# Two LSTM layers on one core: own activations for the gates g and i, biases of g and i copied in by ScalarE

## The reference

```python
def step(carry, xp_t):
    prev_h, prev_c = carry
    h_bar = xp_t + prev_h @ Wh                 # xp = x @ Wx + b
    i = jax.nn.sigmoid(h_bar[:, 0:Hdim])
    f = jax.nn.sigmoid(h_bar[:, Hdim:2 * Hdim])
    o = jax.nn.sigmoid(h_bar[:, 2 * Hdim:3 * Hdim])
    g = jnp.tanh(h_bar[:, 3 * Hdim:4 * Hdim])
    next_c = f * prev_c + i * g
    next_h = o * jnp.tanh(next_c)
    return ((next_h, next_c), next_h)
...
x = x + attention(lstm1(x, cond))     # theta, phi, g projections; (theta phi^T / sqrt(128)) g
x = x + ffn(lstm2(x, cond))           # relu(h W1 + b1) W2 + b2
```

## Time and profile before

| | us |
|---|---|
| runs, median of 3 | 435.31 |
| runs, lowest and highest | 435.30, 435.46 |
| profiled execution, first to last instruction (span) | 431.1 |
| TensorE matmul busy in it | 413.9 (96%) |
| VectorE busy | 282.0 (65%) |
| ScalarE busy | 192.1 (45%) |
| TensorE weight loads busy | 301.4 (70%) |

### The profile page before, as it was taken

The page is one execution under the profiler, slowest core; times in us unless marked ns, Lnnn a source line. Parts: engine busy times, 40 slices in busy tenths (PEclk is TensorE's granted clock), DMA queues, the critical chain, the costliest instruction groups (busy, mean ns, idle before and its releaser), DMA issues.

```text
span 431.1 us, 14329 instructions
## 1 busy us (share of the span) xinstructions
PE 413.9 (96%) x5020; PEld 301.4 (70%) x5020; DVE 282.0 (65%) x1702; ACT 192.1 (45%) x1132; POOL 7.8 (2%) x20
## 2 busy tenths in 40 slices
PE   8999999999999999999999999999999999999996
PEld 5767666666766666666689777777777777777775
DVE  6766666666666666666668766666667666666664
ACT  3565444445444444544445433343443434343342
POOL 7000000000000000000000000000000000000000
PEclk9999999999999999999999999999999999999999
DMA  5011011111001111000000100000000000000000
GB/s 180 10 20 20 13 10 18 18 18 18 13 5 18 18 18 18 16 2 14 14 14 2 27 21 6 12 18 20 18 18 0 18 18 18 18 17 1 18 18 12
DMA packets 11694, 8.19 MB, mean 19 GB/s; under 512 B 1097, under 2 KB 11129, under 8 KB 11674
## 3 DMA queue, kind: packets, MB, share of 16 engines
q1 hardware_dynamic: 10874, 6.17, 7.2%
q0 software_dynamic: 512, 1.22, 0.9%
q10 hardware_dynamic: 288, 0.52, 0.4%
HBM read 2.87 MB, written 1.05 MB: 9 GB/s over the span
## 4 chain that ended last, share of the span: by engine, by line
PE 83%; ACT 7%; DVE 5%; issue 3%; DMA 1%; SPq 0%; DVEq 0%
PE fbank L420 19%; PE bankV L400 14%; PE gibank L414 9%; PE bankU L389 6%; PE bankV L414 5%; PE gibank L377 4%; PE bankY L619 4%; PE bankU L612 3%; DVE cell L990 3%; PE bankV L484 3%; ACT scan L802 3%; PE bankY L479 2%; ACT fgate L795 2%; PE gibank L383 2%; PE bankU L512 2%
## 5 line engine op out<-in xcount | busy, mean ns | idle before, releaser
L420 PEld LDWEIGHTS fbank<-ring,whf 128*128 128x128 f32 x508 | 76.6, 188 | 91.7 <-DVE ring L998 88.1
L795 ACT ACTIVATE fgate<-fbank 128x16 f32<-128x16 f32 x254 | 46.5, 183 | 153.5 <-PE fbank L420 153.2
L420 PE MATMUL fbank<-ring,whf 128*128 128x16 f32 x508 | 98.2, 269 | 6.1 <-DVE ring L998 0.7
L987 DVE TENSOR_TENSOR scan<-fgate,cell 128x16 f32<-128x16 f32 x254 | 45.1, 178 | 77.5 <-ACT fgate L795 75.4
L400 PE MATMUL bankV<-warm_x,zeros 128*128 128x512 bf16 x294 | 93.0, 379 | 0.0
L990 DVE TENSOR_TENSOR_SCAN cell<-scan 128x48 f32<-128x48 f32 x256 | 68.2, 267 | 12.0 <-ACT scan L802 1.1
L809 ACT ACTIVATE cell<-cell 128x16 f32<-128x16 f32 x256 | 43.0, 168 | 67.9 <-DVE cell L990 67.8
L998 DVE TENSOR_TENSOR ring<-cell,ogate_h 128x16 f32<-128x16 f32 x256 | 44.7, 174 | 41.8 <-ACT cell L809 41.6
L414 PEld LDWEIGHTS gibank<-h_hi,wh_parts 128*128 128x128 f16 x1016 | 65.4, 117 | 0.0
L414 PE MATMUL gibank<-h_hi,wh_parts 128*128 128x16 f16 x1016 | 62.1, 169 | 0.0
L414 PE MATMUL gibank<-h_lo,wh_parts 128*128 128x16 f16 x1016 | 62.0, 169 | 0.0
(11 more groups left out here) (182 smaller groups left out, 505.6 us busy)
## 6 DMA issues: line engine op xcount, KB each, us to landing
rows_t<-rows SPq DMA_DIRECT2D x16, 128.0 KB
x_rows<-in_x_dram SPq DMA_DIRECT2D x17, 64.0 KB
out_dram<-y_sb SPq DMA_DIRECT2D x16, 64.0 KB
xres<-x2T SPq DMA_DIRECT2D x15, 64.0 KB, 1.9
xin<-x2T SPq DMA_DIRECT2D x14, 64.0 KB, 1.9
w<-in_L_ffn_W_dram POOLq DMA_DIRECT2D x2, 256.0 KB, 4.1
wh<-in_L_cond_Wh_dram ACTq DMA_DIRECT2D x1, 256.0 KB, 2.7
wx<-in_L_cond_Wx_dram ACTq DMA_DIRECT2D x1, 256.0 KB, 3.6
```

The source lines that it names most:

```text
L420: nc.tensor.matmul(step_out(p, t, GF), whf[layer][:], ring[:, (s - 1) % STEPS, :], start=False, stop=True, skip_group_check=True).then_inc ...
L795: nc.scalar.activation(fgate[:], fbank[p][:, NB * t:NB * t + NB], ACT.Sigmoid, scale=1.0 / Z_UNIT).then_inc(f_done[layer], 1)
L987: nc.vector.tensor_tensor(out=fc_slots, in0=fgate[:], in1=c_psum, op=ALU.mult).then_inc(scan_inputs[layer], 1)
```

## The change

The gates g and i get banks of their own (`gbank`, `ibank`), each with both halves in it. ScalarE does a tanh for g and a sigmoid for i, with a semaphore from TensorE for each (`g_ready`, `i_ready`), and the tanh of c has no scale. The scan runs over two elements for each sequence: slots hold 0 and g to multiply by, i and f*c to add, so that state = 0 * state + i, then state = g * i + f c. Nothing is doubled in the set-up any more.

Since both halves of g and i are in one bank, their biases come as those of o did: TensorE spreads them once for each layer into 128 columns, ScalarE keeps them (`seeds`) and copies three of them in for the other half at t = 0 (`seed`). TensorE waits for the last of the three (`seeded`) at t = 1, now behind the f matmul and ahead of the passes of g. The projections of g and i wait for `o_done` as that of o does; in layer 1 that of o moves from t = 3 to t = 4, where a filler goes. `WARM2` has 9 fillers for each chunk in place of 14.

```diff
-    WARM2 = [0, 2, 1, 2, 2, 2, 2, 3]
+    WARM2 = [0, 2, 1, 1, 2, 2, 1, 1]
+    SEEDED = [GG, GI, GO]
@@ tiles
-        gibank = [ps("gibank0"), ps("gibank1")]
-        cell = ps("cell")
+        gbank, ibank, cell = ps("gbank"), ps("ibank"), ps("cell")
-        c_scan, tanhc = cell[:, 0:3 * NB], cell[:, 3 * NB:4 * NB]
-        scan_mul, scan_add = scan[:, 0:3 * NB], scan[:, 3 * NB + 1:6 * NB + 1]
-        gi_slots = scan[:, 2:6 * NB + 2].rearrange("p (g b k) -> p g b k", g=2, k=3)[:, :, :, 0]
+        c_scan, tanhc = cell[:, 0:2 * NB], cell[:, 2 * NB:3 * NB]
+        scan_mul, scan_add = scan[:, 0:2 * NB], scan[:, 2 * NB:4 * NB]
+        g_slots = scan_mul.rearrange("p (b k) -> p b k", k=2)[:, :, 1]
+        i_slots = scan_add.rearrange("p (b k) -> p b k", k=2)[:, :, 0]
+        fc_slots = scan_add.rearrange("p (b k) -> p b k", k=2)[:, :, 1]
+        def shared_cols(p, g):
+            if g == GO:
+                return bankV[:, (2 + p) * P:(3 + p) * P]
+            return (gbank if g == GG else ibank)[:, p * P:(p + 1) * P]
@@ TensorE, step
+                if after_seeds is not None:
+                    pe.wait_ge(seeded, after_seeds)
                 pe.wait_ge(hi_ready[layer], count)
-                passes(h_hi, [GG, GI])
+                passes(h_hi, GG, (0, 1))
+                passes(h_hi, GI, (0,))
                 pe.wait_ge(lo_ready[layer], count)
-                passes(h_lo, [GG, GI]).then_inc(gi_ready[layer], 1)
+                passes(h_lo, GG, (0, 1)).then_inc(g_ready[layer], 1)
+                passes(h_hi, GI, (1,))
+                passes(h_lo, GI, (0, 1)).then_inc(i_ready[layer], 1)
-                if seeded is not None:
-                    pe.wait_ge(o_seeded, seeded)
@@ TensorE, layer 1 beside the steps
-                if t in (0, 1):
-                    for g in (GATES[0:1], GATES[1:3])[t]:
-                        bias_gate(int(last), 1 - p, g)
+                if t == 0:
+                    bias_gate(int(last), 1 - p, GF)
                 if s == 1 and first:
                     pe.wait_ge(o_done[0], 2)
-                    bias_gate(0, 1, GO).then_inc(o_bias_ready, 1)
+                    for g in SEEDED:
+                        bias_gate(0, 1, g).then_inc(bias_spread, 1)
+                if t in (3, 4):
+                    for g in (SEEDED[0:2], SEEDED[2:3])[t - 3]:
+                        pe.wait_ge(seeded, i * 2 + (p + 1))
+                        pe.wait_ge(o_done[0], i * STEPS + (s + 1))
...
-                elif t not in (0, 3) and not (first and s == 1):
+                elif t not in (0, 3, 4) and not (first and s == 1):
                     add_zeros(1 + (t == 1), 0, i * STEPS + (s + 1))
@@ TensorE, layer 1, step 7 of the first turn
-                    nc.tensor.matmul(bankU[:, 0:P], bias[1][:, gate_cols(GO)], ones[:], start=True, stop=True
-                                     ).then_inc(o_bias_ready, 1)
+                    for k, g in enumerate(SEEDED):
+                        nc.tensor.matmul(bankU[:, k * P:(k + 1) * P], bias[1][:, gate_cols(g)], ones[:],
+                                         start=True, stop=True).then_inc(bias_spread, 1)
@@ TensorE, loop of layer 2
-                    if t in (2, 3, 6):
-                        g = {2: GF, 3: GG, 6: GI}[t]
-                        bias_gate(1, 1 - p, g)
-                        project_gate(1, 1 - p, g, xin[:, 1 - p, :])
-                    if t == 7:
-                        pe.wait_ge(o_seeded, c + (NCH + 1))
+                    if t == 2:
+                        bias_gate(1, 1 - p, GF)
+                        project_gate(1, 1 - p, GF, xin[:, 1 - p, :])
+                    if t in (3, 6, 7):
+                        pe.wait_ge(seeded, c + (NCH + 1))
                         pe.wait_ge(o_done[1], i * STEPS + (s + 1))
-                        project_gate(1, 1 - p, GO, xin[:, 1 - p, :]).then_inc(x2_projected, 1)
+                        last = project_gate(1, 1 - p, {3: GG, 6: GI, 7: GO}[t], xin[:, 1 - p, :])
+                        if t == 7:
+                            last.then_inc(x2_projected, 1)
@@ ScalarE
-                act.wait_ge(gi_ready[layer], n1)
-                nc.scalar.activation(gi_slots,
-                                     gibank[p][:, 2 * NB * t:2 * NB * (t + 1)].rearrange("p (g b) -> p g b", g=2),
-                                     ACT.Tanh, scale=0.5 / Z_UNIT).then_inc(scan_inputs[layer], 1)
+                act.wait_ge(g_ready[layer], n1)
+                nc.scalar.activation(g_slots, shared_cols(p, GG)[:, NB * t:NB * t + NB],
+                                     ACT.Tanh, scale=1.0 / Z_UNIT).then_inc(scan_inputs[layer], 1)
+                act.wait_ge(i_ready[layer], n1)
+                nc.scalar.activation(i_slots, shared_cols(p, GI)[:, NB * t:NB * t + NB],
+                                     ACT.Sigmoid, scale=1.0 / Z_UNIT).then_inc(scan_inputs[layer], 1)
...
-                nc.scalar.activation(tanhc, c_psum, ACT.Tanh,
-                                     scale=0.5).then_inc(h_inputs[layer], 1)
+                nc.scalar.activation(tanhc, c_psum, ACT.Tanh).then_inc(h_inputs[layer], 1)
-            def seed_o(layer, p):
-                nc.scalar.copy(bankV[:, (3 - p) * P:(4 - p) * P], o_bias[layer][:]).then_inc(o_seeded, 1)
+            def seed(layer, p):
+                for k, g in enumerate(SEEDED):
+                    last = nc.scalar.copy(shared_cols(1 - p, g), seeds[layer][:, k, :])
+                last.then_inc(seeded, 1)
@@ VectorE, set-up and step
-            nc.vector.tensor_scalar(wh[0][:, gate_cols(GG)], wh[0][:, gate_cols(GG)], 2.0, None,
-                                    ALU.mult).then_inc(wh_ready, 1)
...
-                dve.wait_ge(scan_inputs[layer], n * 2 + 2)
+                dve.wait_ge(scan_inputs[layer], n * 3 + 3)
                 nc.vector.tensor_tensor_scan(out=c_scan, data0=scan_mul, data1=scan_add, initial=0.0,
                                              op0=ALU.mult, op1=ALU.add).then_inc(c_ready[layer], 1)
```

More of the change, by code:

```diff
@@ L95, in build @@
         ogate_h = sb("ogate_h", [P, NB])
-        o_bias = [sb(f"o_bias{n}", [P, P]) for n in (1, 2)]
+        seeds = [sb(f"seeds{n}", [P, 3, P]) for n in (1, 2)]
         wh_parts = [sb(f"wh_parts{n}", [P, 2, 4 * H], f16) for n in (1, 2)]
@@ L109, in build @@
         ogate = sb("ogate", [P, NB])
-        scan = sb("scan", [P, 98])
+        scan = sb("scan", [P, 4 * NB])
         h_hi = sb("h_hi", [P, STEPS, NB], f16)
@@ L356, in gate_out, with bias_gate @@
             def gate_out(p, g):
[L358 to L362, removed]
-            def step_out(p, t, g):
[L366 to L379, removed]
+                return fbank[p][:, 0:P] if g == GF else shared_cols(p, g)
+            def step_out(p, t, g):
+                return gate_out(p, g)[:, NB * t:NB * t + NB]
+            def bias_gate(layer, p, g, start=False):
+                return nc.tensor.matmul(gate_out(p, g), bias[layer][:, gate_cols(g)], ones[:],
+                                        start=start or g == GF, stop=False, skip_group_check=True)
             def project_gate(layer, p, g, tile):
-                return nc.tensor.matmul(gate_out(p, g), wx[layer][:, gate_cols(g)], moving(tile, g),
+                return nc.tensor.matmul(gate_out(p, g), wx[layer][:, gate_cols(g)], tile,
                                         start=False, stop=False, skip_group_check=True)
@@ L406, in top_product, with step, passes @@
                 nc.tensor.matmul(out, ones[:], w_diag[:], start=True, stop=True).then_inc(top_ready[layer], 1)
-            def step(layer, s, count, o_parts=None, seeded=None):
+            def step(layer, s, count, o_parts=None, after_seeds=None):
                 p, t = s // CH, s % CH
[L411 to L416, removed]
+                def passes(h, g, parts):
+                    for part in parts:
+                        last = nc.tensor.matmul(step_out(p, t, g), wh_parts[layer][:, part, gate_cols(g)],
+                                                h[:, (s - 1) % STEPS, :],
+                                                start=False, stop=True, skip_group_check=True)
                     return last
@@ L530, in beside1 @@
                             project_gate(0, 1 - p, g, rhs(i, p))
-                if s == 5 and first:
-                    pe.wait_ge(scale_made[1], 5)
-                keep_warm(bankU, WARM1[t])
                 if t == 6:
@@ L830, in beside1 @@
                 if first and s == 1:
-                    keep_bias(0, bankV[:, 3 * P:4 * P])
+                    for k in range(3):
+                        last_kept = keep_seeds(k)
+                    last_kept.then_inc(seeded, 1)
                 if first and s == 7:
-                    keep_bias(1, bankU[:, 0:P])
+                    act.wait_ge(bias_spread, 6)
+                    nc.scalar.copy(seeds[1][:].rearrange("p k n -> p (k n)"), bankU[:, 0:3 * P]
+                                   ).then_inc(seeds2_kept, 1)
```

(4 more changed lines are left out.)

126 lines of the change are left out of this document (51 added, 75 removed).

## The result

The changed kernel took 432.54 us, the median of 19 runs from 426.54 to 438.77; the kernel before took 435.39 on the same chips (19 runs, 434.13 to 440.96). Of the runs within 1.5% of each kernel's fastest, the ratio is 0.989, interval 0.987 to 0.992. The sign was right, but the measured -2.9 us is half of the forecast -5.9, and the two kernels differ in something that a median hides: before spreads over 7 us, after over 12. (`WARM2` of the changed kernel sums to 10 fillers for each chunk, not the 9 named ahead of the prediction.)

A forecast was written before the change was run, and what follows sets the result against it. Bound taken: 256 recurrence steps of 1.60 us one after the other, with TensorE waiting for them. Terms -8.1 + 0 + 4.3 - 3.2 + 1.1 = -5.9 us, from 435.3 to 429.4 us; range 425.5 to 434.8.

The forecast's parts named there:

- Scan: VectorE's scan of 32 elements in place of 48 saves 0.033 us in about 245 steps: -8.1 us, ends -4.2 and -9.
- Split tanh: ScalarE's shared tanh split into tanh g and sigmoid i costs 0, with 0.01 us to spare; ends +5 and -2 us.
- ends within 0.01 us of each other: Before each scan, the g and i branch and VectorE's f*c product both end at 102.21, so added branch time shows.
- Seeds' wait: At t = 1, TensorE's g passes wait for three ScalarE copies, 0.14 us late in 31 steps: +4.3 us, ends 0 and +10.
- t = 7 of layer 2: One filler in place of three on TensorE takes the step from 1.83 to 1.60 us, 14 times: -3.2 us.
- Once: One-time costs in layer 1's steps 1 and 7, from bias spreading and copies: together +1.1 us, ends +0.4 and +1.6.
- rival D: TensorE's clock falls after thin steps, one slow t = 0 step in each of 14 halves: +13 us, 442; chance 0.12.
- B: Sigmoid i ends last: scan 0.02 us later in 225 steps (+4.5), seed waits longer (+1.8); 435.7 at worst; chance 0.15.
- E: No change: ScalarE's seed copies do not overlap, +10 us in place of +4.3, time 435.1; chance 0.06.
- C: More saved: seed wait half as long, shared tanh had been the later branch, 2 us each: 425.4 us; chance 0.12.
- the two spacings of 0.106 and 0.20: Skill rule for ScalarE's short activations and 128-column copies: i ends 0.02 behind f*c, seed waits grow 0.06; sum near -0.5.

The follow-up runs named there:

- the kernel with early fillers: The changed kernel plus zero-adding filler matmuls ahead of the projection's wait, in layer 1 (t = 1, 3) and layer 2 (t = 3, 6, 7): 425.14 us.
- The last kernel: The changed kernel plus a semaphore per seed copy, early fillers, ten start fillers for six, four more fillers in layer 1's last half turn: 419.90 us.

## Why the prediction came out right, and where it was wrong

With the clock left out the change is worth -10.1 us, from a span of 431.1 to 421.0 (the kernel with early fillers), not -5.9. What the medians lie above the undisturbed runs is 9.5 for after (432.5 against 423.0) and 2.3 for before (435.4 against 433.1): -10.1 + 9.5 - 2.3 = -2.9, the measured difference. This is bookkeeping; that the excess is the clock's is shown for the two profiled executions of after (15.7 and 6.0 us, below), not for the runs at the median nor for before. That the measured time lies inside the range is luck: two errors of opposite sign, +7.2 of the clock left out and 4.2 too little for the rest.

*Scan, -8.1.* Right: -7.8 alone, 0.033 us a step, fixed time as for other VectorE operations and 2.2 ns an element.

*Split tanh, 0.* Mis-sized: a step of layer 1 went on to 1.55, not 1.57. The step of the reasoning that failed is "ends within 0.01 us of each other": the shared tanh was the later branch. Counted from the start of the sigmoid of f, medians over 254 steps, it ended at 0.407 and f*c at 0.394, and the scan began at 0.439; the tanh ended behind f*c in 218 of the 254. With the split, i ends at 0.380 and f*c at 0.389, and the scan begins at 0.423; i ends behind f*c in 25 of 254. So the later branch changed, and the scan begins 0.016 earlier; a step is 0.015 to 0.017 shorter, 245 steps: -4 us. No run tried the split alone; the price is what the step of 1.551 has beyond the 1.567 of the short scan. Single rows, rounded to 0.01, could not tell these branches apart; the medians of both lines over all steps would have. One step of after:

```profile
105.12 0.18 ACT L784 ACTIVATE fgate<-fbank 128x16 f32<-128x16 f32 x1 [0.69 <-PE fbank L410]
105.24 0.19 ACT L790 ACTIVATE scan<-gbank 128x16 f32<-128x16 f32 x1
105.32 0.18 ACT L793 ACTIVATE scan<-ibank 128x16 f32<-128x16 f32 x1
105.33 0.17 DVE L970 TENSOR_TENSOR scan<-fgate,cell 128x16 f32<-128x16 f32 x1 [0.19 <-ACT fgate L784]
105.54 0.23 DVE L973 TENSOR_TENSOR_SCAN cell<-scan 128x32 f32<-128x32 f32 x1
```

g and i start 0.08 apart. The spacing rule of the Trainium skill (ScalarE: Activation LUTs, What ACT_TABLE_LOAD costs) would give 0.106 and was too long for these; for the copies of 128 columns its 0.20 was right and my 0.17 was not (next rows).

*Seeds' wait, +4.3.* Near in sum, +3.7, by mistakes that offset each other (it also took 0.03 for what f*c covers, where the term of the tanh had found 0.01). Behind the tanh c that follows the step shown above:

```profile
105.81 0.17 ACT L799 ACTIVATE cell<-cell 128x16 f32<-128x16 f32 x1 [0.21 <-DVE cell L973]
105.89 0.26 ACT L815 COPY gbank<-seeds 128x128 f32<-128x128 f32 x1
106.08 0.27 ACT L815 COPY ibank<-seeds 128x128 f32<-128x128 f32 x1
106.28 0.27 ACT L815 COPY bankV<-seeds 128x128 f32<-128x128 f32 x1
106.60 0.11 PEld L404 LDWEIGHTS gbank<-h_hi,wh_parts 128*128 128x128 f16 x2
106.60 0.21 PE L404 MATMUL gbank<-h_hi,wh_parts 128*128 128x16 f16 x2
```

The load starts 0.79 after tanh c, 0.23 later than before (0.56), not 0.17. But matmul and load then start together, where the load had led by 0.11 (99.91; before, same step):

```profile
100.02 0.24 PE L414 MATMUL gibank<-h_hi,wh_parts 128*128 128x16 f16 x4
```

So the first matmul stands 0.79 after tanh c for 0.67, and the step is longer by the same 0.12 only: 31 x 0.12 = 3.7.

*t = 7 of layer 2, -3.2.* Right: -3.6 alone, and in the changed kernel 13 steps go from 1.83 to 1.90 to 1.55, 13 x (0.31 - 0.05) = -3.4, beside the 0.05 that every step gains.

*Once, +1.1.* Right: the step to 2 takes +0.45 and that to 8 +0.62. In addition one step in the first turn of each loop is 0.23 to 0.26 longer than its like in other turns, with the scan waiting for nothing that the trace shows (kernel with early fillers):

```profile
43.37 0.17 DVE L980 TENSOR_TENSOR scan<-fgate,cell 128x16 f32<-128x16 f32 x1 [0.41 <-ACT fgate L794]
43.84 0.23 DVE L983 TENSOR_TENSOR_SCAN cell<-scan 128x32 f32<-128x32 f32 x1 [0.29 <-DVE scan L980]
```

Its cause is open. What other single steps and the end of the run gain about offsets these two.

*Clock, rival D, given 0.12.* This is what failed: the sum holds nothing for the clock, and D priced it as a thing of every half turn or of none. It happens in some. D had 0.93 us for each, put into the step t = 0; measured, it is 0.87 to 1.00, in the steps to t = 1 and t = 2 (4.10 to 4.23 together in place of 3.23), and t = 0 still takes 1.55. Seven in the profiled execution come to 6.8 us, the end of layer 1 to 2.1, the slow start to 6.8: together the 15.7 by which its span exceeds 421.0. In the next execution profiled (span 427.0) there were four falls in layer 2, 4.0 us, and 2.0 at the end of layer 1. The two steps, half turn after half turn (profiled execution of after; in an undisturbed half turn the pair is 1.68, 1.55):

```
half turn  4     5     6     7     8     9 to 11  12    13    14
t=0->1    2.27  2.26  2.22  2.13  2.06  1.68     2.15  2.07  1.68
t=1->2    1.83  1.93  2.01  2.10  2.17  1.55     2.08  2.16  1.55
```

From one fall to the next the second step grows by 0.07 to 0.10 us and the first one shrinks, and then the falls stop for some half turns. The other profile has nearly the same pairs, 2.14 and 2.09, then 2.07 and 2.16, twice. It looks as if the loop slid past something in the chip that does not run in step with it, so that how a run begins decides how many falls it gets; this is my reading, and no experiment tried it. That thin steps are what makes falls possible in layer 2 is shown: with early fillers at t = 3, 6 and 7 there was none there in any of five profiles. Which of the three are needed was not tried; the fillers of t = 3 were always there with the others.

*B and E* fell: the i branch is not last (VectorE's f*c is, by 0.009 in the medians), and the copies do overlap. *C* was right on the shared tanh and wrong on the copies; even its 425.4 was more than the 423.0 of the undisturbed kernel.

Two sums of the prediction do not come out of its own terms. B's first part with half of the second is 429.4 + 4.5 + 0.9 = 434.8, not 433.5, and the two spacings of 0.106 and 0.20 with B's prices give -5.9 + 4.5 + 1.8 = +0.4, not -0.5. Neither changes the forecast.

## What to carry to other kernels

A filler matmul, or an instruction that only happens to keep TensorE busy, can be work that the clock stands on: before taking it away, look which steps become thin (here t = 6 and t = 7, next to each other), price what one fall costs, and expect it in some executions only, so that a single profile can mislead. Put the fillers ahead of a wait, where they fill idle time; here they delayed nothing. Where two branches end within rounding, compare medians over all steps, and take the profiled execution's time, not the median, as the base.

## What the runs showed that I had not expected

The granted clock is shown as 1.00 in the first 24 us also where the matmuls there run at half their rate (0.43 apart for 0.22). The traces' lists of clock levels tell why: the first entry, of 1.00, stands at 4.7 to 5.5 us in the executions with a quick start and at 10.7 to 27.0 us in those whose first steps are long (23.7 in after), and what lies ahead of it is counted as 1.00. So the mean over a run does not tell of a slow start; the spacing in the first steps does. Hence a mean of 1.00 is no proof of an undisturbed run: the kernel with early fillers took 422.96 us at that mean and also 429.88, a difference of 6.9, near the 6.8 of the slow start above, though that run has no profile to show it. Layer 2's fillers alone gave such a run with a profile: 430.39 us at a mean of 1.00, with first steps of 4.32 and 2.82.

The kernel before may have some of the same: 433.1 us in its best runs at clock 1.000, 437.97 to 440.69 in runs at 0.992 to 0.996, none of which has a profile. The last kernel, with ten fillers at the start, early ones in the thin steps and at the end of layer 1, and own waits, is the only one whose six runs all agree within 0.7 us.

After a wait, a weight load and its matmul started at the same time (106.60 above), so that only half of a delay of the load reached the step.
